# Start-up loads and clears in order of use, and a layer's first convolution ahead of its second inverse transform

## The chip, the cores and the metric

The kernel runs on one core of a Trainium2 chip. The metric is the device time of one execution in microseconds (us); the median of three runs is compared.

## The reference

The network takes 64 images of 64x64 points with three numbers each. Its first stage, the tower, is what the change touches; the two behind it (retention attention over the rows, and a mixture of 64 experts) stay as they are.

```python
x = coords @ fc0_w + fc0_b                    # 3 -> 32 channels
for sw, cw, cb in four layers:
    x_ft = rfft2(x, norm='ortho')[:, :, :20, :20]
    x1 = irfft2(einsum('bixy,ioxy->boxy', x_ft, sw), s=(64, 64), norm='ortho')
    x2 = einsum('bchw,oc->bohw', x, cw) + cb  # the 1x1 convolution
    x = gelu(x1 + x2)
h = gelu(x @ fc1_w + fc1_b) @ fc2_w + fc2_b
h = h + attention(layernorm(h))
h = h + experts(layernorm(h))
```

## The kernel before, in words

Everything is float32. The work is written out by hand: each engine has one program (`@block.sync` for the SP queue, `@block.tensor` for PE, `@block.vector` for DVE, `@block.scalar` for ACT), its order is the order of the code, and semaphores are the only tie between engines. A wait stops everything behind it on its engine.

**Start-up.** SP issues five tables (`consts`: the matrices of the forward and inverse transforms and a mask), two 1 MB loads of the input as the first transform needs it (`x_turned` into `turned_w`, quarters 0 and 1), and waits for `zeroed`, since the next loads write blocks into tiles that DVE clears. Then it issues 26 small loads (`blocks`: weights and biases, L349) and two 1 MB loads of the input as the first convolution needs it (`x` into `xin`, L351). DVE clears `fc0_cols`, `w2` and the whole of `modes` (20480 numbers per partition, L633), signals `zeroed`, and clears all eight PSUM banks (`slots`, L635). PE and DVE both wait for all 31 of these loads through the one semaphore `const_in`, and PE for the second clear too. Then PE multiplies `fc0_cols` by the first layer's convolution weights (L491, eight matmuls, 16 records in the trace), DVE copies the product to `first_w` (L640), and only then PE starts on the input.

**The first forward transform.** The input has four channels, so its transform is done on four quarters rather than 32 image pairs: `dft_w(q)` on PE (L394), `turn_w(q)` on DVE (L605), `dft_h(q)` on PE (L406), `turn_h(q)` on DVE (L611), then eight `lift` steps on PE (L421) that make 32 channels of four, each copied into `modes` by ACT (L683). The last eight lifts end the stage.

**A layer.** `mix(l)` multiplies the 20x20 modes by the layer's weights in ten steps (L441); ACT and DVE copy the sums back into `modes`. Then come 32 image pairs: DVE turns a pair's modes (`turn_modes`, L619), PE does `inverse_h` (L454) into banks 4 to 7, DVE turns these (`turn_inverse`, L629), PE does `conv` (L474) into banks 0 to 3 from the layer's input and adds `inverse_w` (L482) to the same banks in four parts, and ACT applies gelu (L696) and stores the pair (L700). The next layer's forward transform of earlier pairs (`turn_act`, `dft_w`, `turn_w`, `dft_h`, `turn_h`) is woven in between from the third pair on. Layer 3 has no next layer and so none of that. At a layer's head PE runs `inverse_h(0)`, waits for the turn of pair 0 (`inv_turned`), runs `inverse_h(1)`, then `conv(0)` and `inverse_w(0)`:

```python
inverse_h(l, 0)
for j in range(PAIRS + (0 if last else 3)):
    if j + 1 < PAIRS:
        ...
            pe.wait_ge(inv_turned, after_inv_turned(l, j, 1))
        inverse_h(l, j + 1)
    if j < PAIRS:
        ...
        conv(l, j)
        for p in range(2):
            inverse_w(l, j, p)
```

Of the kernel before, what the change touches and what calls it, by code (L numbers as in the profile page):

```python
# [15 lines left out]
CH = 32  # L16
MODES = 20
# [9 lines left out]
HID = 64  # L27
IN_CH = 4
# [160 lines left out]
def tower(nc, banks, h_dram, x, x_turned, fc0, fc0_t, sw, cwt, cb, fc1_w, fc1_b, fc2_w, fc2_b,  # L189
# [4 lines left out]
    with ExitStack() as ctx:  # L194
# [3 lines left out]
        def sem(name):  # L198
# [41 lines left out]
        const_in = sem("const_in")  # L240
# [30 lines left out]
        consts = [(fwd_w, k_fwd_w), (fwd_h, k_fwd_h), (inv_h, k_inv_h), (inv_w, k_inv_w), (mask, k_lift_mask)]  # L271
        blocks = [(fc0_rows[:, :], fc0)]
        blocks += [(fc0_cols[:, e, :, e, :],
                    fc0_t.rearrange("c (a k) -> c a k", a=1).broadcast_to([CH, 4, IN_CH]))
                   for e in range(LIFT_E)]
        blocks += [(conv_w[p * CH:(p + 1) * CH], cwt.rearrange("l c o -> c l o")) for p in range(4)]
        blocks += [(conv_b[p * CH:(p + 1) * CH], cb) for p in range(4)]
        blocks += [(w1[p * CH:(p + 1) * CH], fc1_w) for p in range(4)]
        blocks += [(w2[u * HID:(u + 1) * HID, u:u + 1], fc2_w) for u in range(2)]
        blocks += [(b1[u * HID:(u + 1) * HID], fc1_b.rearrange("(c a) -> c a", a=1)) for u in range(2)]  # L280
        blocks += [(b2[:, :], fc2_b.rearrange("(a c) -> a c", a=1).broadcast_to([128, 1]))]
        CONSTS = 16 * (len(consts) + len(blocks))
# [37 lines left out]
        def _(sp):  # L320
# [22 lines left out]
            for dst, src in consts:  # L343
                sp.dma_start(flat(dst[:]), src).then_inc(const_in, 16)
            for q in range(2):
                sp.dma_start(flat(turned_w[:, q]), x_turned[q]).then_inc(xturned_in[q], 16)
            sp.wait_ge(zeroed, 1)
            for dst, src in blocks:
                sp.dma_start(dst, src).then_inc(const_in, 16)  # L349
            for q in range(2):  # L350
                sp.dma_start(flat(xin[:, q]), x[q]).then_inc(xin_in[q], 16)  # L351
            for q in range(2, QUARTERS):
                sp.wait_ge(w_done, q - 1)
                sp.dma_start(flat(turned_w[:, q % 2]), x_turned[q]).then_inc(xturned_in[q % 2], 16)
            for k in range(RING_W):
                load_mode_w(0, k)
            for l in range(LAYERS):
# [29 lines left out]
        def _(pe):  # L387
# [26 lines left out]
            def lift(q, e):  # L414

                n = q * LIFT_E + e
                if n >= 2:
                    pe.wait_ge(lift_out, n - 1)
                for b in range(4):
                    rows_b = slice(b * 32, (b + 1) * 32)  # L420
                    mm = nc.tensor.matmul(banks[rows_b, 2 + n % 2, 0:400], lift_w[rows_b, e, :],  # L421
                                          in_modes[rows_b, 2 * q:2 * q + 2, :, 0:MODES], start=True, stop=True)
                mm.then_inc(lifted, 1)
# [36 lines left out]
            def conv(l, t):  # L460

                pe.wait_ge(inv_turned, after_inv_turned(l, t, 1))
                if t > 0:
                    pe.wait_ge(act_set, after_out(l, t - 1, 3))
# [22 lines left out]

            pe.wait_ge(const_in, CONSTS)
            pe.wait_ge(zeroed, 2)
            for e in range(LIFT_E):  # L490
                mm = nc.tensor.matmul(banks[:, 0, e * CH:(e + 1) * CH],  # L491
                                      fc0_cols[:, e].rearrange("c p e k -> c (p e k)"), conv_w[0:CH, 0, :],
                                      start=True, stop=True)
            mm.then_inc(first_w_filled, 1)
            pe.wait_ge(lift_w_set, 1)
            pe.wait_ge(first_w_set, 1)

            pe.wait_ge(xturned_in[0], 16)
            dft_w(0)
            for q in range(QUARTERS):  # L500
# [7 lines left out]
                if q > 0:  # L508
                    for e in range(LIFT_E):
                        lift(q - 1, e)  # L510
            pe.wait_ge(modes_set, QUARTERS)
            for e in range(LIFT_E):
                lift(QUARTERS - 1, e)

            for l in range(LAYERS):
# [3 lines left out]
                for j in range(PAIRS + (0 if last else 3)):  # L519
                    if j + 1 < PAIRS:  # L520
# [6 lines left out]
                    if j < PAIRS:  # L527
                        if j >= 4 and not last:
                            pe.wait_ge(modes_set, forward(l + 1, j - 4) + 1)
                        conv(l, j)  # L530
# [44 lines left out]
        def mix_part(k, half):  # L575
# [4 lines left out]
            return dst, src  # L580

        @block.vector
        def _(dve):
# [86 lines left out]
            for n in range(IMAGES):  # L670
# [3 lines left out]
                dve.wait_ge(fc2_done, n + 1)  # L674
                nc.vector.tensor_scalar(rows[:, n % (2 * QB), :], banks[:, n % 2 * 4, :], b2[:, 0:1], None,  # L675
# [3 lines left out]
        def _(act):  # L679
            act.wait_ge(const_in, CONSTS)  # L680
# [5 lines left out]
            for l in range(LAYERS):  # L686
                for k in range(MIXES):
# [593 lines left out]
```

## Time and profile before

| what | value |
|---|---|
| median of three runs | 1904.94 us (1903.27 to 1911.12) |
| the profiled execution | 1909.51 us |
| its span, first to last instruction | 1907.7 us |
| around the span | 1.81 us |
| PE busy | 1623.8 us (85%) |
| DVE busy | 1310.5 us (69%) |
| ACT busy | 564.3 us (30%) |
| POOL busy | 0.2 us |
| mean granted TensorE clock | 0.953 |

The time is that of the span and 1.81 us around it. The busy times are sums over stages of different kinds, so they do not say by themselves what ends a stage: the program's first 39 us have no PE work at all, the four layers have PE busy nearly throughout, and the stages behind them share the time between PE and DVE.

### The profile page before, as it was taken

To read this page: it belongs to the slowest core of one execution; us is meant where nothing else is said; L and a number is where in the kernel's file an instruction comes from. 1 tells how busy PE (TensorE), PEld (TensorE's weight loads), DVE (VectorE), ACT (ScalarE), POOL (GpSimd) and SP (SyncE) were. 2 spreads that over 40 slices of the span, in tenths; PEclk is the share of its full clock that TensorE was granted. 3 is DMA by queue.
4 is the path that set the end of the run, shared out by engine and by line. 5 is a ranking of instruction groups with operands and counts; after the bars stand their busy time and mean duration, and the time that the engine had idled before them with its cause. 6 is when DMAs were issued, how large, how long until landed. Compare 5 with 4: busy or idle time off the path is not lost. (4 is left out here: it accounts for less than half of the span.)

```text
span 1907.7 us, 43931 instructions
## 1 busy us (share of the span) xinstructions
PE 1623.8 (85%) x19696; PEld 949.2 (50%) x19696; DVE 1310.5 (69%) x1465; ACT 564.3 (30%) x750; POOL 0.2 (0%) x4
## 2 busy tenths in 40 slices
PE   1989999988999998999999989998767637289994
PEld 0365555557555554755555567766111137233332
DVE  4269888876999997498888845553222254788887
ACT  0332222223222222232222224444676710200000
POOL 0000000000000000000000000000000000000000
PEclk9999999999999999899999999999999975689996
DMA  3233232244755555365555629998555310100000
GB/s 101 93 124 127 119 134 112 112 179 138 258 225 224 222 222 199 105 253 222 222 222 222 229 73 331 355 334 338 196 180 182 117 29 1 69 1 0 0 0 22
DMA packets 62273, 299.94 MB, mean 157 GB/s; under 512 B 21968, under 2 KB 22928, under 8 KB 28048
## 3 DMA queue, kind: packets, MB, share of 16 engines
q1 hardware_dynamic: 43664, 163.01, 25.3%
q10 hardware_dynamic: 18432, 134.23, 16.9%
q8 instruction: 152, 2.49, 0.5%
q14 instruction: 25, 0.20, 0.0%
HBM read 160.90 MB, written 136.31 MB: 156 GB/s over the span
## 5 line engine op out<-in xcount | busy, mean ns | idle before, releaser
L482 PEld LDWEIGHTS slots<-inv_w,inv_out 128*128 128x128 f32 x4096 | 501.4, 197 | 183.6 <-issue 183.6
L696 ACT ACTIVATE act_c<-slots,conv_b 128x512 f32<-128x512 f32 x512 | 352.7, 689 | 752.4 <-PE slots L482 752.4
L482 PE MATMUL slots<-inv_w,inv_out 128*128 128x128 f32 x4096 | 543.0, 288 | 0.0
L629 DVE STREAM_TRANSPOSE inv_out<-slots 128x1024 f32<-128x1024 f32 x256 | 304.0, 1226 | 111.8 <-PE slots L454 111.8
L605 DVE STREAM_TRANSPOSE turned_h<-slots 128x1024 f32<-128x1024 f32 x200 | 237.8, 1227 | 33.4 <-PE slots L394 32.9
L594 DVE STREAM_TRANSPOSE turned_w<-act_c 128x1024 f32<-128x1024 f32 x192 | 225.1, 1210 | 0.0
L394 PE MATMUL slots<-turned_w,fwd_w 32*64 32x512 f32 x3200 | 201.2, 610 | 10.8 <-DVE turned_h L605 10.2
L1163 DVE TENSOR_TENSOR ex_weighted<-slots,ex_y_t 128x512 f32<-128x512 f32 x256 | 157.8, 682 | 33.1 <-PE slots L1033 33.1
L675 DVE TENSOR_SCALAR turned_h<-slots,b 128x512 f32<-128x512 f32 x64 | 48.0, 750 | 165.1 <-PE slots L570 165.1
L707 ACT ACTIVATE inv_out<-slots,b 128x1024 f32<-128x1024 f32 x128 | 135.5, 1111 | 65.9 <-PE slots L561 65.9
L406 PE MATMUL slots<-turned_h,fwd_h 64*64 64x320 f32 x1600 | 137.2, 457 | 5.9 <-DVE modes L611 5.9
L611 DVE STREAM_TRANSPOSE modes<-slots 128x640 f32<-128x640 f32 x96 | 81.3, 847 | 87.2 <-PE slots L406 87.2
L474 PE MATMUL slots<-act_c,conv_w 32*32 32x512 f32 x3072 | 113.5, 613 | 22.6 <-DVE modes L611 15.3
L561 PE MATMUL slots<-act_c,w 32*64 32x512 f32 x1024 | 73.1, 626 | 62.0 <-DVE turned_h L675 57.1
L1045 PE MATMUL slots<-ex_weighted,ex_lattice_w 128*64 128x512 f32 x512 | 123.1, 604 | 0.0
L454 PE MATMUL slots<-turned_k,inv_h 32*64 32x320 f32 x2048 | 102.8, 458 | 18.8 <-DVE inv_out L629 10.2
L619 DVE STREAM_TRANSPOSE turned_k<-modes 128x640 f32<-128x640 f32 x128 | 103.0, 807 | 0.1
L394 PEld LDWEIGHTS slots<-turned_w,fwd_w 32*64 32x64 f32 x3200 | 60.3, 132 | 79.1 <-issue 68.2
L441 PE MATMUL slots<-modes,mode_w 64*64 64x128 f32 x1600 | 90.9, 271 | 3.5 <-DVE modes L611 2.9
L441 PEld LDWEIGHTS slots<-modes,mode_w 64*64 64x64 f32 x1600 | 90.0, 133 | 6.4 <-DVE modes L611 5.1
L651 DVE COPY modes<-slots 128x640 f32<-128x640 f32 x40 | 33.0, 825 | 73.2 <-PE slots L441 73.2
L406 PEld LDWEIGHTS slots<-turned_h,fwd_h 64*64 64x64 f32 x1600 | 51.4, 132 | 53.7 <-issue 9.8
(117 smaller groups left out, 760.6 us busy)
## 6 DMA issues: line engine op xcount, KB each, us to landing
act_scratch<-act_c ACTq DMA_DIRECT2D x128, 1024.0 KB, 4.8
act_c<-act_scratch SPq DMA_DIRECT2D x128, 1024.0 KB, 5.0
mode_w<-in_sw_dram SPq DMA_DIRECT2D x40, 320.0 KB, 2.9
turned_w<-in_x_turned_dram SPq DMA_DIRECT2D x4, 1024.0 KB, 5.2
xin<-in_x_dram SPq DMA_DIRECT2D x4, 1024.0 KB, 6.6
h_scratch<-turned_h SPq DMA_DIRECT2D x256, 4.0 KB
ex_select_raw<-in_k_select_dram SPq DMA_DIRECT2D x1, 2048.0 KB, 8.8
at_h<-h_scratch SPq DMA_DIRECT2D x4, 256.0 KB, 4.5
```

Source lines behind the costliest of these rows:

```text
L394: mm = nc.tensor.matmul(banks[i * 64:(i + 1) * 64, 4 + p, :], fwd_w[p * 32:(p + 1) * 32, wh, :], turned_w[p * 32:(p + 1) * 32, n % 2, wh, ...
L406: mm = nc.tensor.matmul(banks[kwh * 64:(kwh + 1) * 64, i, 0:320], fwd_h[i * 64:(i + 1) * 64, parity, ph, :], turned_h[i * 64:(i + 1) * 64, ...
L441: mm = nc.tensor.matmul(mix_sums(rows_b, k)[:, at:at + 128], mode_w[rows_b, n % RING_W, m, :], modes[rows_b, :, k, 2 * m:2 * m + 2], start ...
L474: nc.tensor.matmul(banks[q * 32:(q + 1) * 32, p, :], w, src, start=True, stop=False, skip_group_check=True)
L482: mm = nc.tensor.matmul(banks[:, p, at:at + 128], inv_out[:, t % 2, i, p, :, :, r].rearrange("p b o -> p (b o)"), inv_w[:, i, :], start=Fa ...
L594: last = nc.vector.transpose(dst, src)
L605: nc.vector.transpose(dst, src).then_inc(w_turned, 1)
L629: nc.vector.transpose(dst, src).then_inc(inv_turned, 1)
L696: nc.scalar.activation(act_c[:, t % RING, :, p, :], banks[:, p, :].rearrange("p (i m) -> p i m", i=2), ACT.Gelu, bias=conv_b[:, l:l + 1]). ...
L707: nc.scalar.activation(unit[:, n % 2, 2 * half:2 * half + 2, :], banks[:, at:at + 2, :], ACT.Gelu, bias=b1[:, 0:1]).then_inc(unit_set, 1)
L1045: mm = nc.tensor.matmul(slots[j * D:(j + 1) * D, SLOTS - 1, 0:512], lattice_w[:, n, :], weighted[:, n % WB, j * 512:(j + 1) * 512], start= ...
L1163: nc.vector.tensor_tensor(weighted[:, n % WB, cols], slots[:, n % PB, cols], y_t[:, bass.ds(g * SLOT + half * 512, 512)], ALU.mult).then_i ...
```

## The change

The one semaphore for all constants becomes three (`fwd_in`, `lift_in`, `rest_in`), each waited for where its data are used, and SP issues the loads in another order. DVE's clear of `modes` becomes a clear of its 12 pad columns alone (640 runs of 12 numbers per partition), on POOL, with a semaphore `pads_zeroed`; the clear of the PSUM banks is dropped. The product for `first_w` moves from the head of PE's program to ahead of the last eight lifts, and uses bank 4. `conv(l, 0)` moves ahead of `inverse_h(l, 1)` in each of the four layers, and does not wait for `inv_turned`.

```diff
+        lift_consts = [(mask[:, :], k_lift_mask), (fc0_rows[:, :], fc0)]
+        lift_consts += [(conv_w[p * CH:(p + 1) * CH], cwt.rearrange("l c o -> c l o")) for p in range(4)]
+        lift_consts += [(fc0_cols[:, e, :, e, :],
+                         fc0_t.rearrange("c (a k) -> c a k", a=1).broadcast_to([CH, 4, IN_CH]))
+                        for e in range(LIFT_E)]
+        rest = [(flat(inv_h[:]), k_inv_h), (flat(inv_w[:]), k_inv_w)]
...
-            for dst, src in consts:
-                sp.dma_start(flat(dst[:]), src).then_inc(const_in, 16)
-            for q in range(2):
-                sp.dma_start(flat(turned_w[:, q]), x_turned[q]).then_inc(xturned_in[q], 16)
+            sp.dma_start(flat(fwd_w[:]), k_fwd_w).then_inc(fwd_in, 16)
+            sp.dma_start(flat(turned_w[:, 0]), x_turned[0]).then_inc(xturned_in[0], 16)
+            sp.dma_start(flat(fwd_h[:]), k_fwd_h).then_inc(fwd_in, 16)
+            sp.dma_start(flat(turned_w[:, 1]), x_turned[1]).then_inc(xturned_in[1], 16)
             sp.wait_ge(zeroed, 1)
-            for dst, src in blocks:
-                sp.dma_start(dst, src).then_inc(const_in, 16)
-            for q in range(2):
-                sp.dma_start(flat(xin[:, q]), x[q]).then_inc(xin_in[q], 16)
+            for dst, src in lift_consts:
+                sp.dma_start(dst, src).then_inc(lift_in, 16)
             for q in range(2, QUARTERS):
                 sp.wait_ge(w_done, q - 1)
                 sp.dma_start(flat(turned_w[:, q % 2]), x_turned[q]).then_inc(xturned_in[q % 2], 16)
+            for dst, src in rest:
+                sp.dma_start(dst, src).then_inc(rest_in, 16)
             for k in range(RING_W):
                 load_mode_w(0, k)
+            for q in range(2):
+                sp.dma_start(flat(xin[:, q]), x[q]).then_inc(xin_in[q], 16)
...
                 if n >= 2:
                     pe.wait_ge(lift_out, n - 1)
+                else:
+                    pe.wait_ge(lift_w_set, 1)
...
-                pe.wait_ge(inv_turned, after_inv_turned(l, t, 1))
                 if t > 0:
+                    pe.wait_ge(inv_turned, after_inv_turned(l, t, 1))
                     pe.wait_ge(act_set, after_out(l, t - 1, 3))
...
-            pe.wait_ge(const_in, CONSTS)
-            pe.wait_ge(zeroed, 2)
-            for e in range(LIFT_E):
-                mm = nc.tensor.matmul(banks[:, 0, e * CH:(e + 1) * CH],
...
-            mm.then_inc(first_w_filled, 1)
-            pe.wait_ge(lift_w_set, 1)
-            pe.wait_ge(first_w_set, 1)
-
+            pe.wait_ge(fwd_in, 32)
             pe.wait_ge(xturned_in[0], 16)
...
+            for e in range(LIFT_E):
+                mm = nc.tensor.matmul(banks[:, 4, e * CH:(e + 1) * CH],
...
+            mm.then_inc(first_w_filled, 1)
             pe.wait_ge(modes_set, QUARTERS)
             for e in range(LIFT_E):
                 lift(QUARTERS - 1, e)
+            pe.wait_ge(rest_in, REST)
+            pe.wait_ge(first_w_set, 1)
...
                 for j in range(PAIRS + (0 if last else 3)):
+                    if j == 0:
+                        conv(l, 0)
                     if j + 1 < PAIRS:
...
-                        conv(l, j)
+                        if j > 0:
+                            conv(l, j)
...
+        @block.gpsimd
+        def _(pool):
+            nc.gpsimd.memset(modes[:, :, :, MODES:32], 0.0).then_inc(pads_zeroed, 1)
+
...
-            nc.vector.memset(modes[:], 0.0)
             dve.drain().then_inc(zeroed, 1)
-            nc.vector.memset(banks[:, :, :], 0.0).then_inc(zeroed, 1)
-            dve.wait_ge(const_in, CONSTS)
+
+            turn_w(0)
+            dve.wait_ge(lift_in, LIFT)
             nc.vector.tensor_tensor(lift_w[:], across(fc0_rows[:, :], LIFT_E), along(mask[:, :], CH),
                                     ALU.mult).then_inc(lift_w_set, 1)
-            dve.wait_ge(first_w_filled, 1)
-            nc.vector.tensor_copy(flat(first_w[:]), banks[:, 0, 0:LIFT_E * CH]).then_inc(first_w_set, 1)
-
-            turn_w(0)
             for q in range(QUARTERS):
                 if q + 1 < QUARTERS:
                     turn_w(q + 1)
                 turn_h(q, in_modes[:, 2 * q:2 * q + 2])
+            dve.wait_ge(first_w_filled, 1)
+            nc.vector.tensor_copy(flat(first_w[:]), banks[:, 4, 0:LIFT_E * CH]).then_inc(first_w_set, 1)
+            dve.wait_ge(pads_zeroed, 1)
```

ACT waits for `rest_in` ahead of its first copy of layer 0's mix, instead of for `const_in` at its head.

How the instructions stand in the built programs, at the places of which the prediction speaks. First the SP queue at the program's start, before:

```order
L1219 DMA ident<-in_k_ident_dram 128x128
L344 DMA fwd_w<-in_k_fwd_w_dram 128x128
L344 DMA fwd_h<-in_k_fwd_h_dram 128x256
L344 DMA inv_h<-in_k_inv_h_dram 128x128
L344 DMA inv_w<-in_k_inv_w_dram 128x256
L344 DMA lift_mask<-in_k_lift_mask_dram 128x8
L346 DMA turned_w<-in_x_turned_dram 128x2048 x2
L349 DMA fc_rows<-in_fc_dram 128x32
L349 DMA fc_cols<-in_fc_t_dram 32x4x4 x8
L349 DMA conv_w<-in_cwt_dram 32x4x32 x4
```

and the SP queue at the same place with the change:

```order
L1234 DMA ident<-in_k_ident_dram 128x128
L347 DMA fwd_w<-in_k_fwd_w_dram 128x128
L348 DMA turned_w<-in_x_turned_dram 128x2048
L349 DMA fwd_h<-in_k_fwd_h_dram 128x256
L350 DMA turned_w<-in_x_turned_dram 128x2048
L353 DMA lift_mask<-in_k_lift_mask_dram 128x8
L353 DMA fc_rows<-in_fc_dram 128x32
L353 DMA conv_w<-in_cwt_dram 32x4x32 x4
L353 DMA fc_cols<-in_fc_t_dram 32x4x4 x8
L356 DMA turned_w<-in_x_turned_dram 128x2048 x2
L358 DMA inv_h<-in_k_inv_h_dram 128x128
```

The first quarter of the input now stands third in the queue instead of seventh, 14 small loads stand between quarters 1 and 2, and the other 15 behind quarter 3.

PE from the program's start to the mix of layer 0, before:

```order
L491 MATMUL slots<-conv_w,fc_cols 128x32 x8
L394 MATMUL slots<-turned_w,fwd_w 64x512 x32
L406 MATMUL slots<-turned_h,fwd_h 64x320 x8
...
L421 MATMUL slots<-act_c,lift_w 32x400 x64
L441 MATMUL slots<-modes,mode_w 64x128 x200
```

and with the change:

```order
L400 MATMUL slots<-turned_w,fwd_w 64x512 x32
L412 MATMUL slots<-turned_h,fwd_h 64x320 x8
...
L429 MATMUL slots<-act_c,lift_w 32x400 x32
L511 MATMUL slots<-conv_w,fc_cols 128x32 x8
L429 MATMUL slots<-act_c,lift_w 32x400 x32
L449 MATMUL slots<-modes,mode_w 64x128 x200
```

The eight matmuls for `first_w` went from the head to between the last two groups of eight lifts.

PE at the head of layer 1 (layers 0, 2 and 3 are alike), before:

```order
L441 MATMUL slots<-modes,mode_w 64x128 x200
L454 MATMUL slots<-turned_k,inv_h 64x320 x16
L474 MATMUL slots<-act_c,conv_w 32x512 x16
L482 MATMUL slots<-inv_w,inv_out 128x128 x16
L454 MATMUL slots<-turned_k,inv_h 64x320 x8
```

and with the change:

```order
L449 MATMUL slots<-modes,mode_w 64x128 x200
L462 MATMUL slots<-turned_k,inv_h 64x320 x8
L482 MATMUL slots<-act_c,conv_w 32x512 x16
L462 MATMUL slots<-turned_k,inv_h 64x320 x8
L490 MATMUL slots<-inv_w,inv_out 128x128 x16
```

The 16 matmuls of the first convolution now stand between the inverse transforms of pairs 0 and 1.

## Rows read from the trace of the kernel before

**Rows 1.** The page's section 1: busy time and share of the span.

```profile
PE 1623.8 (85%) x19696; PEld 949.2 (50%) x19696; DVE 1310.5 (69%) x1465; ACT 564.3 (30%) x750; POOL 0.2 (0%) x4
```

**Rows 2.** Stretches: length, busy and instructions by engine, granted clock, DMA share, GB/s.

```profile
0.00:39.19 39.19, 0.00 (x0) 0.00 (x0) 21.57 (x5) 0.00 (x0) 0.20 (x4) 1.00 0.26 74
...
43.37:88.55 45.18, 40.19 (x448) 10.62 (x448) 12.56 (x12) 16.95 (x33) 0.00 (x0) 0.96 0.25 88
...
150.00:400.00 250.00, 243.53 (x3374) 145.08 (x3374) 224.31 (x212) 73.07 (x106) 0.00 (x0) 1.00 0.30 119
```

**Rows 3.** Timeline of SP's queue: start, length of the issue, line, transfer.

```profile
1.19 0.41 SPq L344 DMA_DIRECT2D fwd_w<-in_k_fwd_w_dram  x1
...
3.54 0.91 SPq L346 DMA_DIRECT2D turned_w<-in_x_turned_dram  x2
...
23.72 3.75 SPq L349 DMA_DIRECT2D fc_cols<-in_fc_t_dram  x8
...
34.37 1.88 SPq L349 DMA_DIRECT2D b<-in_fc_b_dram  x3
```

**Rows 4.** DMA issues at the start: size each, us from issue to landing.

```profile
turned_w<-in_x_turned_dram SPq DMA_DIRECT2D x1, 1024.0 KB, 5.5
...
turned_w<-in_x_turned_dram SPq DMA_DIRECT2D x1, 1024.0 KB, 7.4
...
fwd_h<-in_k_fwd_h_dram SPq DMA_DIRECT2D x1, 128.0 KB, 2.3
...
fc_cols<-in_fc_t_dram SPq DMA_DIRECT2D x8, 2.0 KB, 2.5
```

**Rows 5.** Timeline of DVE and PE, start to the first quarter's turn.

```profile
1.00 0.91 DVE L631 MEMSET fc_cols<- 32x1024 f32 x1 [1.00 <-PEq L1273]
...
6.17 17.12 DVE L633 MEMSET modes<- 128x20480 f32 x1 [4.21 <-issue]
...
39.19 3.62 PE L491 MATMUL slots<-conv_w,fc_cols 32*128 32x32 f32 x16 [39.19 <-DMA b<-in_fc_b_dram]
...
43.37 3.72 PE L394 MATMUL slots<-turned_w,fwd_w 32*64 32x512 f32 x32 [0.56 <-issue]
...
47.19 2.38 DVE L605 STREAM_TRANSPOSE turned_h<-slots 128x1024 f32<-128x1024 f32 x2 [3.92 <-PE slots L394]
```

**Rows 6.** The first transforms of quarters 1 and 2, and the clock between.

```profile
49.71 2.72 PE L394 MATMUL slots<-turned_w,fwd_w 32*64 32x512 f32 x32 [2.62 <-DVE turned_h L605]
...
55.01 1.98 PE L394 MATMUL slots<-turned_w,fwd_w 32*64 32x512 f32 x32 [0.44 <-DVE turned_h L605]
```

**Rows 7.** The same stretch by fives of us, columns as in rows 2.

```profile
50.00:55.00 5.00, 4.57 (x48) 1.23 (x33) 2.52 (x3) 0.00 (x0) 0.00 (x0) 0.66 0.58 185
```

**Rows 8.** Timeline of PE at the head of layer 0, and DVE's third turn.

```profile
112.54 0.80 PE L454 MATMUL slots<-turned_k,inv_h 32*64 32x320 f32 x16 [1.80 <-DVE turned_k L619]
...
115.88 1.38 PE L454 MATMUL slots<-turned_k,inv_h 32*64 32x320 f32 x16 [2.54 <-DVE inv_out L629]
...
117.18 2.04 PE L474 MATMUL slots<-xin,first_w 32*32 32x512 f32 x32
...
119.15 4.04 PE L482 MATMUL slots<-inv_w,inv_out 128*128 128x128 f32 x32
...
124.02 2.38 DVE L629 STREAM_TRANSPOSE inv_out<-slots 128x1024 f32<-128x1024 f32 x2 [3.56 <-PE slots L454]
```

**Rows 9.** Timeline of PE: the same place in layers 1 and 2.

```profile
453.58 2.06 PE L474 MATMUL slots<-act_c,conv_w 32*32 32x512 f32 x32
...
455.57 4.66 PE L482 MATMUL slots<-inv_w,inv_out 128*128 128x128 f32 x32
...
795.88 5.12 PE L482 MATMUL slots<-inv_w,inv_out 128*128 128x128 f32 x32
```

**Rows 10.** Timeline of POOL: two of its four memsets.

```profile
0.23 0.10 POOL L1273 MEMSET const-float32-0.0<- 128x1 f32 x1 [0.23 <-issue]
0.27 0.10 POOL L1273 MEMSET const-float32-1.0<- 128x1 f32 x1
```

More of the change, by code:

```diff
@@ L237, in tower @@
             "p k (a n) -> p k a n", a=4)
-        const_in = sem("const_in")
+        fwd_in = sem("fwd_in")
+        lift_in = sem("lift_in")
+        rest_in = sem("rest_in")
+        pads_zeroed = sem("pads_zeroed")
         zeroed = sem("zeroed")
@@ L269, in tower @@
         h_out = [sem(f"h_out{b}") for b in range(2)]
[L271 to L282, printed above, removed]
+        lift_consts = [(mask[:, :], k_lift_mask), (fc0_rows[:, :], fc0)]
[4 more added lines that the diff above has]
+        rest = [(flat(inv_h[:]), k_inv_h), (flat(inv_w[:]), k_inv_w)]
+        rest += [(conv_b[p * CH:(p + 1) * CH], cb) for p in range(4)]
+        rest += [(w1[p * CH:(p + 1) * CH], fc1_w) for p in range(4)]
+        rest += [(w2[u * HID:(u + 1) * HID, u:u + 1], fc2_w) for u in range(2)]
+        rest += [(b1[u * HID:(u + 1) * HID], fc1_b.rearrange("(c a) -> c a", a=1)) for u in range(2)]
+        rest += [(b2[:, :], fc2_b.rearrange("(a c) -> a c", a=1).broadcast_to([128, 1]))]
+        LIFT = 16 * len(lift_consts)
+        REST = 16 * len(rest)
         block = ctx.enter_context(nc.Block())
@@ L486, in inverse_w @@
                 mm.then_inc(summed, 1)
-            pe.wait_ge(const_in, CONSTS)
-            pe.wait_ge(zeroed, 2)
-            for e in range(LIFT_E):
-                mm = nc.tensor.matmul(banks[:, 0, e * CH:(e + 1) * CH],
-                                      fc0_cols[:, e].rearrange("c p e k -> c (p e k)"), conv_w[0:CH, 0, :],
-                                      start=True, stop=True)
-            mm.then_inc(first_w_filled, 1)
-            pe.wait_ge(lift_w_set, 1)
-            pe.wait_ge(first_w_set, 1)
+            pe.wait_ge(fwd_in, 32)
             pe.wait_ge(xturned_in[0], 16)
@@ L510, in _ @@
                         lift(q - 1, e)
+            for e in range(LIFT_E):
+                mm = nc.tensor.matmul(banks[:, 4, e * CH:(e + 1) * CH],
+                                      fc0_cols[:, e].rearrange("c p e k -> c (p e k)"), conv_w[0:CH, 0, :],
+                                      start=True, stop=True)
+            mm.then_inc(first_w_filled, 1)
             pe.wait_ge(modes_set, QUARTERS)
@@ L674, in _ @@
                 dve.wait_ge(fc2_done, n + 1)
+                if n == 0:
+                    dve.wait_ge(rest_in, REST)
                 nc.vector.tensor_scalar(rows[:, n % (2 * QB), :], banks[:, n % 2 * 4, :], b2[:, 0:1], None,
@@ L679, in _ @@
         def _(act):
-            act.wait_ge(const_in, CONSTS)
             for n in range(PAIRS):
@@ L686, in _ @@
             for l in range(LAYERS):
+                if l == 0:
+                    act.wait_ge(rest_in, REST)
                 for k in range(MIXES):
```

## The prediction

> **What bounds the kernel now.** I read the page's busy times first: PE is busy for 85% of the span [rows 1]. The table by stretches says where it is not [rows 2]. For the first 39.19 us PE does nothing. From 43.37 to 88.55, the transform of the input, it is busy for 40.2 of 45.2 us, and inside layer 0 for 243.5 of 250. So the layers follow PE and the DVE turns it alternates with; the start follows something else.
>
> The timelines tell what. SP issues its first loads by 4.5 us, then stands still: the small loads come around 23.7, and the last of them at 34.37 + 1.88 = 36.3 [rows 3]. It waited for DVE's clear of `modes`. That row gives 17.12 us of work and 4.21 us of "issue" before it [rows 5]; together 21.33 us for 20480 numbers, 1.04 ns each, so I read both as the clear itself, from 1.96 (where the gap begins) to 23.3. PE's first matmul, at 39.19, waited for the last small load; it is the `first_w` product, 3.62 us, and the first transform of the input starts at 43.37 [rows 5]. Its data had been there for long: the two quarters, issued at 3.54 and about 4.0, landed 5.5 and 7.4 us later, at 9.0 and 11.4 [rows 3, 4]. Some 34 us are lost between.
>
> At a layer's head PE runs `inverse_h(0)` from 112.54 to 113.34, idles 2.54 us until DVE has turned it, and then has three things in a row: `inverse_h(1)`, `conv(0)`, `inverse_w(0)` [rows 8]. The convolution needs nothing of the turn.
>
> **The change part by part.**
>
> *First transform.* Quarter 0 is issued third, at about 1.66, behind `ident` and `fwd_w`; issues are 0.47 us apart. At 4.9 us from issue to landing, the best of the four such loads, it lands at 6.6; at 5.5 at 7.2 [rows 4]. `fwd_h`, now also waited for, is behind it in the queue with 128 KB; alone it took 2.3 us, and behind 1 MB I add its share, 0.2 us. If the queue served quarter 1 beside quarter 0, both would land at 2.6 + 7.4 = 10.0. I take 7.4, nearest to the first quarter's own row, and keep 6.6 and 10.0. The start moves by 43.37 - 7.4 = **36.0 us** earlier. The Trainium skill (DMA: Bandwidth & Descriptors, Anatomy of one DMA) gives about 2.0 us plus bytes at 436 GB/s, an estimate of 4.4 us for 1 MB; by it the sum would be 1 us larger, and the rows, slower by 0.5 to 1 us, speak for mine.
>
> *The clears.* `fc0_cols` (from 1.00, 0.91 us) and the tiny `w2` are done at 1.96 [rows 5], so `zeroed` comes while SP still issues quarter 1. The 14 small loads of the lift are issued from 3.1 to 9.6 (14 x 0.47) and land by 12.5, with 2.5 us each [rows 4] and quarter 1 in front. DVE waits for them behind `turn_w(0)`, which ends at 7.4 + 3.8 + 2.4 = 13.6 [rows 5]: no wait. The product `lift_w` (0.4 us) lies in DVE's idle time while PE does quarter 1. SP goes on to quarter 2 when `dft_w(0)` is done, at 11.2; it lands at 16.4, and PE wants it at 19. Quarter 3 is issued near 17 and the other 15 small loads, five mode loads and two `xin` loads until about 28; the mix comes after 50. All **0**. The cover is the 45 us of the input stage: only what outlasts it would be seen.
>
> *The clock.* Between 50 and 55 us the mean granted clock is 0.66, full speed and half speed by turns, after PE had stood idle for 2.6 us [rows 6, 7]; the first transform takes 3.72 us, the second 2.72, the third 1.98 [rows 5, 6]. With no `first_w` product ahead of it, the first will take 3.72 as now and the second, I think, 3.72 too: **1.0 us** back. Ends: nothing, and 3.6, if the third transform and what lies around it are also at half speed (1.75 for that transform, as much again half way around it).
>
> *`first_w`.* The 16 matmul records took 3.62 us with PE fresh from idleness. At full speed I take half, **1.8 us**, in the PE chain of the lifts. Ends 0 (ACT's copies of the lifts catch up meanwhile) and 3.6. DVE's copy of the product is behind its last turn and ahead of the last eight lifts, so before its reader.
>
> *The first convolution.* It took from 117.18 to 119.15, 1.97 us, in layer 0 and 1.99 from 453.58 to 455.57 in layer 1; layers 2 and 3 show 1.99 each [rows 8, 9]. In the 2.54 us gap even the slow version (2.06) fits, since PE is free from 113.34 and the turn ends at 115.8. So 4 x 1.99 = **8.0 us**. Does it last? `turn_inverse(1)` on DVE does not move, but the next one has 3.56 us of idle time before it, waiting for PE [rows 8]; PE is in front and all behind it moves by the 2 us. In layers 1 to 3 the input pair is loaded by DMA long before.
> Besides, PE is less idle there. `inverse_h(1)` took 1.38 against 0.80, and `inverse_w(0)` 4.04, 4.66 and 5.12 us in layers 0, 1 and 2 for the same work [rows 8, 9]. All at the faster figures would give 0.58 (layer 0), 0.62 (1), 0.58 + 1.08 (2) and 0.62 (3, like 1), 3.5 us. I take half, **1.8**, and keep 0 and 3.5. The Trainium skill (TensorE: Matmul & The Clock Gate, What's actually happening) has the rate set by how busy PE has recently been. These rows agree, and by that rule alone I would count all 3.5 here and the cold start above.
>
> *Sum.* 36.0 - 1.0 - 1.8 + 8.0 + 1.8 = 43.0 us. The profiled execution took 1909.51 (span 1907.7 and 1.81 around it), so 1866.5. It was 4.57 us above the median of the runs, 1904.94; by the median I forecast **1862 us**.
>
> **The rivals.**
>
> *Late data and a cold PE*: quarters at 10.0 (2.6 later) and the clock's worse end (2.6 more): 1862 + 5 = 1867; with `first_w` at half speed 1869. Chance 0.15.
>
> *POOL stands in DVE's way.* POOL's clear and DVE's of `fc0_cols` both want SBUF at 1 us. If DVE's had to wait for POOL's, `zeroed` would come when POOL is done. For POOL the trace has only memsets of one number [rows 10]; at DVE's 1.04 ns, 7680 numbers are 8.0 us, at twice that 16. With `zeroed` at 9, the lift's loads land at 18.4 and DVE's second turn, ready at 17.4, is 1.5 late; at 17, the loads land at 26.4 and quarter 2, issued behind them, at 29, where PE wants it at 20: 9 late. So 1864 to 1871. Against: DVE's clear runs at 1.04 ns a number, one at a time. Chance 0.08. The Trainium skill (SBUF — State Buffer, SBUF: two separate sides) says that DVE and GpSimd share a port pair that one holds for its whole instruction, but only against a DVE operation in a two-port mode or with two SBUF inputs; no row before shows the two together.
>
> *The convolution moves and gives nothing*, since something else then holds `inverse_w(0)`: 1862 + 9.8 = 1872. The rows show nothing else. Chance 0.04.
>
> *Slower: POOL's clear outlasts its cover.* DVE waits for `pads_zeroed` ahead of its first copy of the mix, which comes about 2.5 us into the mix, at 88.55 + 2.5 - 33.2 = 58 us, and PE's third step of the mix waits for that copy. POOL's memset of a single number lasts 0.10 us [rows 10]. If each of the 640 runs of 12 cost that, the clear ends at about 65 us and takes 7 us of the gain (1869); if each of the 7680 numbers did, it would end at 768 and the time would be 1862 + 710 = 2572. It decides from 58 + 43 = 101 us on, 13 ns a number, 12 times DVE's rate. Two such memsets start 0.04 us apart [rows 10], so 0.10 is a fixed part, not a rate. Chance 0.03 of slower; 0.02 goes to ends in the band around no change.
>
> **How the numbers follow.** The forecast, within 1855 and 1867, has 0.68. The low end is a landing at 6.6 (-0.8), a warm second transform (-1.0), `first_w` half hidden (-0.9), the clock's 1.7 more at the layers' heads, and runs 1.7 under the median (1903.27 against 1904.94): together 6, and 1 for what I price too high. The high end takes in the first rival and most of the second. Range **1855 to 1871**. A measurement of this kernel can tell about 0.5%, 9.5 us: faster by more 0.95, within 0.02, slower 0.03.
>
> **What would show it.** PE's first row at 7 to 8 us instead of 39.19, the mix of layer 0 starting near 55 instead of 88.55; a POOL memset of `modes` that ends before 20 us and no DVE wait for it; no wait for `rest_in`; at each layer's head a convolution between the two inverse transforms, PE's idle time there about 0.5 to 1.4 us instead of 2.54, and `inverse_w` starting 2 us sooner after it. The step length inside the layers and all behind them should stay. Wrong it would be if PE's start stood beyond 12 us, if DVE idled at the lift's weights, or if the input stage took over 50 us instead of 45.

## The result and the profile after

| | before | with the change |
|---|---|---|
| median | 1905.15 us (4 runs, 1903.27 to 1911.12) | 1864.68 us (4 runs, 1858.20 to 1867.38) |
| ratio | | 0.976 (95% interval 0.9731 to 0.9789) |
| profiled execution | 1909.51 us, span 1907.7 | 1862.68 us, span 1860.8 |
| forecast | | 1862 us, 1855 to 1871 |

The medians fell by 40.5 us, 2.5 below the forecast's 43.0; by the ratio, which is an estimate of its own over the same runs, it is 46 us, within 40 to 51. The direction, the size and the two places were right. The spans of the two profiled executions differ by 46.9 us; why this is more than the medians show is taken up below.

The page's span and busy times after the change, and its stretches (length, busy and instructions by engine, granted clock, DMA share, GB/s), against [rows 1, 2]:

```profile
span 1860.8 us, 43928 instructions
...
PE 1620.8 (87%) x19696; PEld 950.0 (51%) x19696; DVE 1289.6 (69%) x1463; ACT 564.5 (30%) x750; POOL 6.7 (0%) x5
...
0.00:7.35 7.35, 0.00 (x1) 0.00 (x1) 0.95 (x2) 1.28 (x1) 6.70 (x5) 1.00 0.69 236
7.35:53.69 46.34, 41.86 (x465) 12.47 (x465) 13.41 (x14) 15.77 (x32) 0.00 (x0) 0.96 0.43 148
115.00:365.00 250.00, 243.51 (x3375) 145.07 (x3374) 224.29 (x211) 73.08 (x106) 0.00 (x0) 1.00 0.30 119
```

PE does the same work. The 39 us without PE have become 7.35 us, the input stage is 46.34 instead of 45.18, and inside layer 0 PE is busy for 243.5 of 250 us, to the tenth as before.

The timeline of the start after the change, all engines, against [rows 3, 5, 6]:

```profile
0.73 6.50 POOL L593 MEMSET modes<- 128x7680 f32 x1 [0.29 <-POOLq L1288]
0.73 1.28 ACT L696 ACT_TABLE_LOAD   x1 [0.73 <-PEq L1288]
...
1.01 0.91 DVE L644 MEMSET fc_cols<- 32x1024 f32 x1 [1.01 <-PEq L1288]
...
7.35 3.57 PE L400 MATMUL slots<-turned_w,fwd_w 32*64 32x512 f32 x32 [7.35 <-DMA fwd_h<-in_k_fwd_h_dram]
...
13.58 3.33 PE L400 MATMUL slots<-turned_w,fwd_w 32*64 32x512 f32 x32 [2.66 <-DVE turned_h L618]
14.77 0.43 DVE L650 TENSOR_TENSOR lift_w<-fc_rows,lift_mask 128x256 f32<-128x256 f32 x1 [1.33 <-DMA fc_cols<-in_fc_t_dram]
16.84 1.64 PE L412 MATMUL slots<-turned_h,fwd_h 64*64 64x320 f32 x16
...
19.48 1.98 PE L400 MATMUL slots<-turned_w,fwd_w 32*64 32x512 f32 x32 [1.01 <-DVE turned_h L618]
...
44.97 1.97 PE L511 MATMUL slots<-conv_w,fc_cols 32*128 32x32 f32 x16
...
53.69 22.18 PE L449 MATMUL slots<-modes,mode_w 64*64 64x128 f32 x400 [0.81 <-ACT modes L696]
```

The first transform starts at 7.35 and waited for `fwd_h`; the mix starts at 53.69 instead of 88.55. POOL's clear ends at 7.2, under the cover of all this. DVE's clear beside it takes 0.91 us, as without it.

PE at the heads of layers 0 and 1 after the change, against [rows 8, 9]:

```profile
77.66 0.80 PE L462 MATMUL slots<-turned_k,inv_h 32*64 32x320 f32 x16 [1.79 <-DVE turned_k L632]
78.39 1.73 PE L482 MATMUL slots<-xin,first_w 32*32 32x512 f32 x32
81.00 1.37 PE L462 MATMUL slots<-turned_k,inv_h 32*64 32x320 f32 x16 [0.88 <-DVE inv_out L642]
82.30 5.56 PE L490 MATMUL slots<-inv_w,inv_out 128*128 128x128 f32 x32
...
419.31 1.19 PE L482 MATMUL slots<-act_c,conv_w 32*32 32x512 f32 x32
421.91 0.80 PE L462 MATMUL slots<-turned_k,inv_h 32*64 32x320 f32 x16 [1.42 <-DVE inv_out L642]
```

The convolution fills part of the gap. In layers 1 to 3 PE stays at full speed there; in layer 0 of this profile it does not, and `inverse_w(0)` takes 5.56 us instead of 4.04.

To see where the time went I took the start of the same work in each profile and subtracted it from the start in the profile of before. The lead of each kernel, in us (computed from the timelines' rows; "mix" and "inverse_h" are their first starts in a layer, "pair 1" is the start of the second convolution of a layer, "attention" the first reduction of the stage behind the tower; the other kernels are those of the experiments):

```
place               change  after_third  head_only  conv_only  warm_ends
first transform      36.0       36.4        36.2        0.7       36.2
mix, layer 0         34.9       35.8        34.5        0.8       34.5
pair 1, layer 0      35.3       38.4        34.6        3.3       37.1
inverse_h, layer 1   30.9       34.0        34.6        2.4       37.1
pair 1, layer 1      33.6       36.6        34.6        5.0       39.7
inverse_h, layer 2   33.5       36.6        34.6        3.4       42.5
pair 1, layer 2      37.2       40.2        34.6        7.0       46.1
inverse_h, layer 3   34.3       37.3        33.3        5.7       47.7
pair 1, layer 3      36.9       39.9        32.1        8.3       50.3
attention            46.4       36.5        34.6       17.7       59.3
end                  46.9       36.3        34.5       17.6       59.9
```

The change's column reads: 34.9 from the start; at the four heads +0.5, +2.6, +3.7, +2.6; at the ends of the layers -4.4, 0 and -2.9; behind the head of layer 3 +9.5. The last two were not in the prediction.

### The profile page after: what moved, and what is told of

Its sections match the earlier page's. It is cut to its first block and busy times, and to the rows that moved or that the text cites. A ratio compares the mean times of both kernels' runs of the same rounds, so it can differ in the third digit from the quotient of the medians.

```text
span 1860.8 us, 43928 instructions
## 1 busy us (share of the span) xinstructions
PE 1620.8 (87%) x19696; PEld 950.0 (51%) x19696; DVE 1289.6 (69%) x1463; ACT 564.5 (30%) x750; POOL 6.7 (0%) x5
```

## Experiments

Three questions were open: whether start and convolutions give what their terms say; why layers 0 and 2 give time back at their ends; and what the 9.5 us behind the head of layer 3 are.

### Each kernel once more

`before_again` is the kernel before, `after_again` and `after_third` the change, none with an edit.

> The kernel before once more, for a second profile of it. Theory A (its profiled execution was like any other): median 1905, ratio 1.000, and the profile again shows half-speed stretches at the heads of layers 1 to 3 and a wait of about 4 us for a load of act_c at the start of the stage behind the layers (near 1336 us), with some 1.2 us waits before it. Theory B (that wait is a thing of the single execution): the profile shows no such wait, a span of 1900 to 1904 us, and the kernel's profiled 1909.5 us was the high end of its spread.

> The changed kernel once more. Median 1862 to 1867, ratio 0.976 to 0.980. Theory A (the half-speed stretches of PE at the ends of layers 0 and 2 belong to the changed program): its profile shows them again, mix of layer 1 starting near 393 us. Theory B (they fall differently in each execution): the lead over the kernel before at the mix of layer 1 is not 32.6 us again but anywhere from 32 to 36.

> The change a third time, on the chip of the three below: 1862 to 1866, ratio 0.976 to 0.978.

Measured: before_again 1908.36 us (12 runs, 1899.03 to 1914.3), ratio 0.9998 (0.9976 to 1.0021); after_again 1862.28, ratio 0.9771 (0.9737 to 0.9804); after_third 1863.11, ratio 0.9759 (0.9727 to 0.9791). Where a kernel was run six times or more, the kernel before spread by 14 to 21 us over its executions and the change by 17 to 18, so a pair of profiles tells single terms, not the total.

The waits for the loads of `act_c` from layer 3 on show part of that spread. First the timeline of the kernel before, at the first stage behind the layers, then the list of waits (in all, times, longest) of after_third:

```profile
1336.10 2.01 PE L561 MATMUL slots<-act_c,w 32*64 32x512 f32 x16 [4.00 <-DMA act_c<-act_scratch]
```

```profile
PE slots L482 <- DMA act_c<-act_scratch: 10.6, 8, 2.2
```

The profile of before has 4.1 us of such waits in three convolutions of layer 3, the 4.00 us above, and half speed for the next 9 us. The profile of the change has none, before_again 0.4 us, after_third 10.6 us in eight. There a pair is loaded and another stored per 5.9 us. DMA moved 352 GB/s from 1120 to 1290 us in the change and 331 in after_third (last column):

```profile
1120.00:1290.00 170.00, 165.24 (x2260) 122.50 (x2258) 83.31 (x80) 79.02 (x116) 0.00 (x0) 1.00 0.95 352
```

```profile
1120.00:1290.00 170.00, 156.76 (x2109) 117.78 (x2107) 81.81 (x79) 74.28 (x108) 0.00 (x0) 0.99 0.88 331
```

So theory B held for the wait: it belongs to an execution, and most of the 9.5 us are a wait that the profile of before had and that of the change had not. Why the transfers keep up in one execution and not in the next stays open. Theory B's span, 1900 to 1904 us, did not come: before_again, without that wait, has a span of 1912.5. It lost 11.5 us between the first reduction of the attention stage and the end. The rows of that stretch, before and before_again:

```profile
1539.52:1907.70 368.18, 268.51 (x1248) 147.83 (x1248) 276.76 (x479) 28.78 (x35) 0.00 (x0) 0.82 0.04 14
```

```profile
1532.84:1912.50 379.66, 279.76 (x1248) 158.64 (x1248) 276.82 (x479) 28.77 (x35) 0.00 (x0) 0.79 0.04 13
```

DVE and ACT are busy for the same time; PE takes 11.3 us longer for the same 1248 instructions, at a granted clock of 0.79 instead of 0.82. So this part of the spread is PE at half speed for longer. Over the twelve executions of before_again the mean granted clock goes with the time, from 0.961 at 1899.03 us to 0.947 at 1914.3. The profile of before, at 1909.51, stood 1 to 4 us above the medians of the kernel before (1905.15 to 1908.36), so the median was the better base for the forecast.

For the layers' ends theory A held in after_again (mix of layer 1 at 392.5, lead 33.0, and 31.4 at its first inverse). In after_third the lead at the mix was 35.8, but 2.6 us were lost between pair 1 and there, and 4.4 to the first inverse. All three profiles of the change lose 4.3 to 4.4 us at the end of layer 0. At the end of layer 2 after_again lost only 0.2, and after_third gained 2.6 us at the head of layer 0, where the change's first profile gained 0.5. pads_ten, below, shows that even the end of layer 0 is not fixed by the program.

### The two parts alone

`head_only` is the change with the first convolution back in its place:

```diff
-                    if j == 0:
-                        conv(l, 0)
...
-                        if j > 0:
-                            conv(l, j)
+                        conv(l, j)
```

> The start-up part alone: loads, clears, semaphores and the first_w product as in the change, the first convolution of each layer where it was. By the prediction's terms 36.0 - 1.0 - 1.8 = 33.2 us; the profile of the change showed 34.9 at the mix of layer 0. So 1905 - 34 = 1871 us (1868 to 1874). Rival (the layers give back what they are given, by waits or clock): the same time as the full change, 1864.

`conv_only` is the kernel before with the opposite edit, and `pe.wait_ge(inv_turned, ...)` in `conv` for pairs above 0 only.

> The first convolution alone ahead of the second inverse transform, in each layer; start-up as before. By the prediction's terms 8.0 + 1.8 = 9.8 us: 1895 us (1893 to 1898). Rival (most of it is given back at the layers' ends, as the change's profile shows 7 us less lead there): 1902 to 1905. The mix of layer 0 starts near 88.5 us as before, and inverse_w of pair 0 near 117.2 instead of 119.15.

Measured: head_only 1876.08 us, ratio 0.9829 (0.9798 to 0.986). That is 29.5 us below the median of 1905.6, or 32.6 by the ratio (27 to 38), and 2 us above the range that was expected. conv_only 1894.88, as expected, ratio 0.9938 (0.9915 to 0.996): 10.7 us by the medians, 11.8 by the ratio (8 to 16). One of its eight executions took 7838 us, for no reason that I know, and hardly touches the median. Together 40 us by the medians and 44.4 by the ratios, against 43.3 and 43.6 for both at once (after_again): the parts add, as far as this spread can tell. Both rivals fell, 1864 for head_only and 1902 to 1905 for conv_only, and both terms stand within the noise: 33.2 and 9.8 were forecast. PE at the head of layer 0 in conv_only:

```profile
112.48 1.19 PE L474 MATMUL slots<-xin,first_w 32*32 32x512 f32 x32
115.09 0.80 PE L454 MATMUL slots<-turned_k,inv_h 32*64 32x320 f32 x16 [1.42 <-DVE inv_out L632]
115.82 4.04 PE L482 MATMUL slots<-inv_w,inv_out 128*128 128x128 f32 x32
```

All is at full speed, and the four heads give 2.5, 2.6, 3.6 and 2.6 us, 11.4 in all, against 9.3 in the profile of the change. So layer 0's head can give 2.5. In the profiles of the change and of after_again it gives 0.5, with half speed on it; in after_third, the same program, it is all at full speed and gives 2.6. head_only at the same place runs `inverse_h(1)` and the convolution slowly (1.38 and 1.96 us), like the kernel before.

### PE kept busy in its waits

The ends of the layers in the change, PE:

```profile
382.64 3.66 PE L400 MATMUL slots<-turned_w,fwd_w 32*64 32x512 f32 x32 [2.39 <-DVE turned_h L618]
...
389.57 2.41 PE L412 MATMUL slots<-turned_h,fwd_h 64*64 64x320 f32 x16 [1.99 <-DVE modes L624]
...
392.96 23.80 PE L449 MATMUL slots<-modes,mode_w 64*64 64x128 f32 x400 [0.97 <-DVE modes L624]
```

Behind waits of 2.39, 1.99 and 0.97 us the same work takes 3.66 instead of 1.97, 2.41 instead of 1.36 and 23.80 instead of 22.18, and the granted clock is 0.74 over 380 to 400 us. To test whether PE's idleness has a part in it, PE multiplies a tile of zeros while it would wait. Nothing reads the products. In `warm_ends`:

```diff
+            def fill(count, at):
+                for _ in range(count):
+                    nc.tensor.matmul(at, warm[:, :], warm[:, :], start=True, stop=True)
...
                 mix(l)
+                pe.wait_ge(mix_out["act"], after_mix(l, MIXES - 2))
+                fill(6, banks[:, 1, 384:512])
...
                         elif j >= PAIRS:
+                            if j == PAIRS + 1:
+                                fill(8, banks[:, 3, 0:128])
                             pe.wait_ge(w_turned, after_w_turned(forward(l + 1, j - 3), 1))
...
+                            if j == PAIRS + 2:
+                                fill(6, banks[:, 3, 0:128])
                             pe.wait_ge(modes_set, forward(l + 1, j - 4) + 1)
                         dft_h(forward(l + 1, j - 3), (l + 1) % 2)
+                        if j == PAIRS + 2:
+                            fill(2, banks[:, 3, 0:128])
```

> The change, and the same zero matmuls in PE's waits at the ends of layers 0 to 2 (8 before the transform of the last pair, 6 and 2 around the last dft_h) and 6 behind each mix. Theory A (what layers 0 and 2 give back, 4.4 and 2.9 us in the profile of the change, is half speed after those waits): no stretch at half speed there, dft_w of the last pair 1.97 us, dft_h 1.36, a mix 22.2 us in every layer; the time falls by 5 to 8 us against the change, ratio to the kernel before 0.973 to 0.975. Rival (the zeros lengthen the waits as much as they save): the same time as the change, 0.977.

> The change with zero matmuls at the layers' ends, a second time. Theory A (the gain of its first run is the mechanism's): ratio 0.970 to 0.972, 10 to 13 us below the change, and again no stretch at half speed between the third transform and the end of layer 3. Rival (a lucky execution): within 4 us of the change.

Measured: 1851.62 us, ratio 0.9705 (0.9673 to 0.9738), and the second time 1852.61, ratio 0.9721 (0.9688 to 0.9755), 10.5 us below the change on the same chip (1863.11). That is more than the 5 to 8 us expected of the first. The end of layer 0, and the stretch from 380 to 400 us in warm_ends:

```profile
378.56 2.05 PE L501 MATMUL slots<-warm 128*128 128x128 f32 x16
380.82 1.98 PE L403 MATMUL slots<-turned_w,fwd_w 32*64 32x512 f32 x32 [0.21 <-DVE turned_h L634]
...
386.07 1.36 PE L415 MATMUL slots<-turned_h,fwd_h 64*64 64x320 f32 x16 [0.45 <-DVE modes L640]
...
388.40 22.18 PE L452 MATMUL slots<-modes,mode_w 64*64 64x128 f32 x400 [0.33 <-DVE modes L640]
```

```profile
380.00:400.00 20.00, 19.01 (x298) 15.58 (x298) 9.10 (x11) 3.46 (x5) 0.00 (x0) 1.00 0.73 259
```

The lead no longer falls at the ends of the layers, it rises by 2.8 at the end of layer 1 and by 1.6 at that of layer 2, where the kernel before had lost time itself. Against the change's -4.4, 0 and -2.9 this is almost 12 us, about what the medians show. Theory A holds: none of the five profiles with this filling (those below too) has half speed at a layer's end. The Trainium skill (TensorE: Matmul & The Clock Gate, What's actually happening) has the rate set by how busy PE has recently been; these rows agree, and they show that zeros count as work.

Idleness is not the whole of it, though. pads_ten, the last experiment, leaves the layers' code as it is in the change and delays layer 0 by 12 us. The end of its layer 0:

```profile
392.49 1.98 PE L400 MATMUL slots<-turned_w,fwd_w 32*64 32x512 f32 x32 [2.39 <-DVE turned_h L621]
...
397.73 1.36 PE L412 MATMUL slots<-turned_h,fwd_h 64*64 64x320 f32 x16 [1.97 <-DVE modes L627]
400.06 22.18 PE L449 MATMUL slots<-modes,mode_w 64*64 64x128 f32 x400 [0.97 <-DVE modes L627]
```

The waits are those of the change, and everything is at full speed, as it is at the ends of its layers 1 and 2. The kernel before and head_only have the same waits at full speed there too. So such waits are followed by half speed in some executions and not in others; what decides it these runs do not show. What they show is that it did not come in any of the five profiles in which the waits were filled.

`warm_head` has 12 such matmuls ahead of the first transform and 8 behind it (`fill(12, banks[:, 2, 0:128])`, `fill(8, ...)` for quarter 0); `warm_all` has both.

> The change, and beside it PE multiplies a tile of zeros by itself: 12 matmuls of 128x128 ahead of its wait for the first loads, 8 while DVE turns quarter 0 (results unused). Theory A (the first two transforms are slow only since PE was idle before them): they take about 2.0 us each instead of 3.57 and 3.33, dft_h of quarter 0 1.36 instead of 1.64, and the mix of layer 0 starts 2 to 3 us sooner than the 53.7 us of the change, less what the zeros cost: 1862 instead of 1864. Rival (the granted clock does not answer to zeros, or the zeros are in the way): the mix starts at 54 to 57 us.

> Both fillings. If the two add: 7 to 10 us below the change, 1855 to 1858, ratio 0.972 to 0.974. If only the later one counts, the time of warm_ends.

Measured: warm_head 1863.18 us, ratio 0.9766 (0.9728 to 0.9804); warm_all 1853.34, ratio 0.9709 (0.9677 to 0.9741). The first theory held for the two transforms and not for the stage. PE in warm_head:

```profile
7.10 1.98 PE L403 MATMUL slots<-turned_w,fwd_w 32*64 32x512 f32 x32 [1.65 <-DMA fwd_h<-in_k_fwd_h_dram]
...
11.71 1.98 PE L403 MATMUL slots<-turned_w,fwd_w 32*64 32x512 f32 x32 [0.65 <-DVE turned_h L629]
...
17.80 3.63 PE L403 MATMUL slots<-turned_w,fwd_w 32*64 32x512 f32 x32 [2.83 <-DVE turned_h L629]
```

The first two run at full speed, 3 us are won, and then DVE waits for the lift's loads before it may turn quarter 1: PE idles 2.83 us instead of 1.01, and the third transform runs at half speed, 3.63 us instead of 1.98. The lead at the mix is 34.9 us, to the tenth what it was. A wait that had been hidden came to light, and with the slow transform behind it used up what had been won. Accordingly warm_head takes the change's time, and warm_all, which was to be 7 to 10 us faster if the two fillings added, that of warm_ends: the filling at the start adds nothing that can be measured.

### The first_w product in a gap

In `early_ends` the product stands in PE's wait for DVE's turn of quarter 1, and DVE makes `lift_w` behind that turn; `early_all` has the zeros at the start too:

```diff
+                if q == 1:
+                    pe.wait_ge(lift_in, LIFT)
+                    for e in range(LIFT_E):
+                        mm = nc.tensor.matmul(banks[:, 2, e * CH:(e + 1) * CH],
...
             turn_w(0)
-            dve.wait_ge(lift_in, LIFT)
...
             for q in range(QUARTERS):
                 if q + 1 < QUARTERS:
                     turn_w(q + 1)
+                if q == 0:
+                    dve.wait_ge(lift_in, LIFT)
...
                 turn_h(q, in_modes[:, 2 * q:2 * q + 2])
```

> warm_ends, with the first_w product in PE's wait for DVE's turn of quarter 1 (bank 2) instead of between the lifts, where it took 1.97 us; DVE's product for lift_w behind its turn of quarter 1. If the prediction's term for first_w stands, the mix of layer 0 starts 1 to 2 us sooner than the 54.0 us of warm_ends, 1850 in all. Rival: the product delays the transform of quarter 2 by as much.

> early_ends with the zero matmuls at the start too. In warm_head the first two transforms ran at full speed but DVE then waited for the lift's loads ahead of its turn of quarter 1, and the third transform fell to half speed. With the product in that gap and DVE's order changed: third transform about 2.0 us, mix of layer 0 at 49 to 50.5 us, 3 to 4 us before warm_ends, 1848 in all. Rival: half speed comes at another place of the input stage and the mix starts at 52 or later.

Measured: early_ends 1849.16 us (1848.17 to 1850.32), ratio 0.9692 (0.9665 to 0.9719), the lowest median of all, though its interval overlaps those of warm_ends; early_all 1854.71 (1845.58 to 1858.15), ratio 0.9718 (0.9685 to 0.975). By the profiles, the input stage from the first transform to the mix is 46.9 us in warm_ends, 45.3 in early_ends and 42.5 in early_all, whose mix starts at 49.6 as expected. The stage gained what was expected of early_ends and a little more than that in early_all. The total of early_all, expected at 1848, does not show it. Its profiled execution took 1848.21 with 7.2 us of waits for `act_c` from layer 3 on, where early_ends' has none; four of its six executions took 1853 to 1858, and of those there is no profile. The two intervals overlap. Which of the two is the better program these runs leave open.

### How long the clear on POOL may take

`pads_ten` clears the pads ten times, each waiting for the one before; DVE waits for the tenth.

```diff
-            nc.gpsimd.memset(modes[:, :, :, MODES:32], 0.0).then_inc(pads_zeroed, 1)
+            for n in range(10):
+                if n > 0:
+                    pool.wait_ge(pads_zeroed, n)
+                nc.gpsimd.memset(modes[:, :, :, MODES:32], 0.0).then_inc(pads_zeroed, 1)
...
-            dve.wait_ge(pads_zeroed, 1)
+            dve.wait_ge(pads_zeroed, 10)
```

> The change with POOL's clear of the pad columns done ten times in a row, each behind the one before. At 6.5 us each it ends at about 66 us, when the first DVE copy of layer 0's mix, at 56.2 us in the change, has waited 10 us; PE's third step of the mix waits for that copy. Theory A (the cover is the input stage and ends at 56 us): the time is 8 to 10 us longer than the change's, 1872 to 1875. Rival (the copies of the mix have slack, so nothing is seen): 1864.

Measured: 1870.19 us, ratio 0.9817 (0.977 to 0.9864), 5.5 to 8 us more than the change's three medians. The timeline and the groups:

```profile
66.27 1.56 DVE L666 COPY modes<-slots 128x640 f32<-128x640 f32 x2 [20.16 <-POOL modes L596]
67.24 7.95 PE L449 MATMUL slots<-modes,mode_w 64*64 64x128 f32 x90 [10.23 <-DVE modes L666]
```

```profile
L596 POOL MEMSET modes<- 128x7680 f32 x10 | 65.0, 6499 | 0.8 <-POOLq L1291 0.3
```

PE waits 10.23 us for the copy, and the lead at the first inverse is 22.9 us instead of 34.9. So the rival's mechanism is real, and the cover ends where the prediction put it, within 2 us (58 forecast; without POOL's tenth clear, which ended at 66.2, the copy comes at 56.2). The price of the total is less sure: 1870.19 lies below the 1872 to 1875 expected, and its interval overlaps the change's. The profiled execution took 1863.56, the fastest of the four, and its span is within 1 us of the change's: what it lost at layer 0 it had back by the layers' ends, where the change ran at half speed and it did not. One clear takes 6.5 us, a ninth of the cover.

## Why the prediction was right, point by point

- **First transform at 7.4.** It was 7.35; the two ends, 6.6 and 10.0, were not needed. Quarter 0 landed 5.0 us after its issue, quarter 1 7.5 us after its own, at 10.1. The Trainium skill (DMA: Bandwidth & Descriptors, Anatomy of one DMA), which the prediction weighs here, states its rule for loads that GpSimd issues; this one was issued by SP and took 5.0 us against the rule's estimate of 4.4, so the rows were the better base.
- **The lift's loads by 12.5, no wait.** Wrong, though it cost nothing. DVE waited 1.33 us, to 14.77. The step that failed took 2.5 us from issue to landing out of a quiet stretch [rows 4]; behind quarter 1 in the queue these 14 loads took 3.6 to 6.6 us. The last one, which decides, was issued at 9.7 and landed at 14.7, long after quarter 1 and with quarter 2 (issued at 11.0) under way; which of the two held it is not shown. DVE would have been idle until 16.96 anyway. warm_head shows what it costs when PE is faster.
- **The clock at the start, 1.0 us lost.** The first transform took 3.57 and the second 3.33 us, against 3.72 and 2.72: the second was 0.6 slower where I had 1.0, and `dft_h` behind it 0.6 faster (1.64 against 2.21). The net is near nothing. In after_third the second took 2.62, in pads_ten 1.98, and in head_only the 3.72 that I had: this is not a fixed price. The granted clock reads 1.00 over the first transform, although its 3.57 us, against 1.98 at full speed, say half speed; so early in a trace the durations are the better witness.
- **first_w, 1.8 us.** It took 1.97 in its new place, and early_ends, which hides it, starts the mix 1.6 us sooner from the first transform.
- **Not in the sum.** The input stage grew by 1.2 us where I had 2.8. In the kernel before, ACT's table load (1.28 us) came with the first lift and held up PE:

```profile
59.20 1.28 ACT L683 ACT_TABLE_LOAD   x1 [59.20 <-PE slots L421]
...
61.04 1.21 PE L421 MATMUL slots<-act_c,lift_w 32*32 32x400 f32 x12 [1.28 <-ACT modes L683]
```

  With the wait for `const_in` gone from ACT's head the load comes at 0.73, in nobody's way; head_only has it at 0.74 and conv_only, which keeps that wait, at 58.41. The prediction has no term for that edit.
- **The convolutions, 8.0 + 1.8 us.** 9.3 at the heads in the profile; in conv_only 11.4 at the heads, and 10.7 by the medians or 11.8 by the ratio. Of the 3.5 us that the clock could add, half was about right for the profile of the change, where layer 0's head stayed slow, and all of it for conv_only and after_third.
- **"The step length inside the layers and all behind them should stay."** Inside the layers it did. At their ends it did not: -4.4, 0 and -2.9 us. The change has half speed at all three ends; the kernel before had it in full only at that of layer 1, hence the 0 there. pads_ten has none at these ends, with the same code there. This was the step that the prediction lacked; it looked at the clock only where the change touched the code. That it came out close has a part of luck: warm_ends, which has no such loss, takes 1852, outside the range of 1855 to 1871.
- **The rivals.** POOL in DVE's way: no, DVE's clear took 0.91 us beside POOL's as alone. The Trainium skill (SBUF — State Buffer, SBUF: two separate sides) has the two block each other only if DVE's operation is in a two-port mode or has two SBUF inputs; the trace agrees for this pair. Late data: no. The convolution that gives nothing: no in layers 1 to 3; nearly so in layer 0 in two of three profiles of the change, by the clock and not by a wait. POOL's clear beyond its cover: no; pads_ten shows that the wait would have come where it was put.

## What to carry to other kernels

Ask of every load and clear which instruction first needs it, and give each group its own semaphore: one semaphore for 31 loads made the first matmul wait for the last bias, 34 us late. Half speed comes and goes at places that the change does not touch, so read the granted clock over the whole program, and fill PE's short waits, best with work that has to be done anyway (the product in early_ends), else with zeros. And compare medians of many runs: against the one profile of before, the profiles of the change are ahead by 36 or by 47 us, depending on which execution was caught.

## What the runs showed of the hardware that was not expected

- Matmuls on a tile of zeros, with unread results, keep PE at full speed. Filling three waits of 1 to 2.4 us at each end of layers 0 to 2 and the one behind each mix gave 10 to 13 us of 1864.
- Waits of 2.39, 1.99 and 0.97 us at a layer's end were followed by half speed at all three ends in the change, in full only at one end in the profile of the kernel before, and at none in pads_ten, which has the change's code there. In the steady part of layer 0 the granted clock was 1.00 from 115 to 365 us.
- The kernel before took 1899.03 us at a mean granted clock of 0.961 and 1914.3 at 0.947. In the profile of the latter PE was busy for 11.3 us longer behind the layers, with the same instructions.
- POOL cleared 640 runs of 12 numbers per partition at 0.85 ns a number (6.50 us for 7680); DVE's contiguous clear took 1.04 [rows 5].
- Small loads issued behind 1 MB of the same queue took 3.6 to 6.6 us to land instead of some 2.5.
- With 1 MB loaded and 1 MB stored per 5.9 us, at 331 to 352 GB/s, the loads are in time in one execution and make PE wait 10.6 us in the next. The cause stays open; a deeper ring of `act_c`, which could tell, was not tried.
